# Sparsemax cross-attention on one core: thresholds by Newton steps for eight heads an operation, and score matmuls on a head's own 32 partitions

## The reference, cut to what matters

```python
def sparsemax(x):                       # over the 722 keys
    x = x - max(x); zs = sort_descending(x)
    cssv = cumsum(zs) - 1.0
    k = max(sum(zs > cssv / arange(1, L + 1)), 1)
    tau = cssv[k - 1] / k
    return clip(x - tau, 0.0)

h = layernorm(x)                        # x: 8 x 100 x 512, 16 heads of 32
q, k, v = h @ Wq + bq, ctx @ Wk + bk, ctx @ Wv + bv     # ctx: 8 x 722 x 512
att = sparsemax(q_h @ k_h.T / sqrt(32)) @ v_h           # each head h
x = x + att @ Wo + bo
h = layernorm(x)
x = x + sqrt((h @ cos(theta + theta_noise))**2 + (h @ sin(phi + phi_noise))**2)
```

## Time and profile before

| | us |
|---|---|
| median of 3 runs | 843.59 (840.98 to 843.95) |
| the profiled execution | 843.08 |
| its span, first to last instruction | 840.8 |
| TensorE busy | 657.9 (78%) |
| VectorE busy | 629.0 (75%) |
| ScalarE busy | 454.7 (54%) |
| POOL busy | 181.9 (22%) |

### The profile page before, as it was taken

The page is one execution under the profiler, slowest core; times in us unless marked ns, Lnnn a source line. Parts: engine busy times, 40 slices in busy tenths (PEclk is TensorE's granted clock), DMA queues, the critical chain, the costliest instruction groups (busy, mean ns, idle before and its releaser), DMA issues.

```text
span 840.8 us, 16547 instructions
## 1 busy us (share of the span) xinstructions
PE 657.9 (78%) x4960; PEld 423.0 (50%) x4960; DVE 629.0 (75%) x4046; ACT 454.7 (54%) x872; POOL 181.9 (22%) x147
## 2 busy tenths in 40 slices
PE   3796824778887779898888979997759979995485
PEld 2463613644466445664467536744447446742351
DVE  3699994699936997599929993899629994999401
ACT  2262745554486454874498438854538447842441
POOL 5710530002420034202420152015300152000000
PEclk9898765889889789999899989998979989997698
DMA  9610100000020000200020002000020000000000
GB/s 311 231 49 1 72 1 1 3 2 0 11 92 1 0 11 1 92 0 0 10 93 0 0 10 92 1 0 10 1 91 0 0 10 13 3 1 10 11 2 10
DMA packets 9806, 26.25 MB, mean 31 GB/s; under 512 B 2090, under 2 KB 2090, under 8 KB 8686
## 3 DMA queue, kind: packets, MB, share of 16 engines
q1 hardware_dynamic: 9710, 25.35, 8.7%
HBM read 23.71 MB, written 1.64 MB: 30 GB/s over the span
## 4 chain that ended last, share of the span: by engine, by line
DVE 70%; issue 10%; PE 8%; DMA 5%; DVEq 3%; SPq 2%; ACT 2%; ACTq 0%
DVE cand L743 22%; DVE cand L755 17%; DVE top L750 14%; DMA xq<-in_x 3%; DVE csum L765 2%; PE work L333 2%; PE work L338 2%; PE tps L406 2%; DMA out_y<-att 2%; DVE topz L761 2%; DVE gk L768 1%; SPq L193 1%; DVE g_max L771 1%; DVE st L718 1%; DVEq L830 1%
## 5 line engine op out<-in xcount | busy, mean ns | idle before, releaser
L743 DVE MAX8 cand<-S 100x8 f32<-100x60 f32 (+1 forms) x1536 | 191.0, 205 | 43.5 <-issue 25.4
L406 PE MATMUL tps<-ident,S 100*128 100x100 f32 x768 | 102.9, 276 | 80.6 <-DVEq L835 46.6
L390 PE MATMUL work<-kT,qz 128*100 128x361 f16 x768 | 151.7, 339 | 0.8 <-ACT k_f L565 0.8
L581 ACT ACTIVATE S<-S,neg_tau 100x722 f32<-100x722 f32 x128 | 114.3, 895 | 69.8 <-DVE neg_tau L773 69.8
L755 DVE MATCH_REPLACE8 cand<-top,cand 100x96 f32<-100x96 f32 x640 | 148.1, 243 | 0.0
L750 DVE MAX8 top<-cand 100x8 f32<-100x96 f32 x768 | 139.9, 245 | 0.0
L333 PE MATMUL work<-ctxT,wk 128*128 128x361 f16 x768 | 134.1, 340 | 7.0 <-ACT k_f L565 5.7
L406 PEld LDWEIGHTS tps<-ident,S 100*128 100x128 f32 x768 | 84.7, 155 | 101.2 <-ACT pT L546 44.0
L283 POOL TENSOR_TENSOR ctxT<-ctxT_f,ctxT 128x1024 f16<-128x1024 f32 (+1 forms) x24 | 46.8, 1950 | 393.1 <-ACT ctxT L546 392.8
L333 PE MATMUL work<-wv,ctxT 128*128 128x512 f16 x576 | 125.7, 379 | 0.4 <-ACT S L546 0.4
L546 ACT ACTIVATE S<-work 100x722 f32<-100x722 f32 x128 | 99.4, 776 | 27.9 <-PE work L390 25.4
(11 more groups left out here) (99 smaller groups left out, 586.5 us busy)
## 6 DMA issues: line engine op xcount, KB each, us to landing
ctxT_f<-in_ctx SPq DMA_DIRECT2D x8, 1444.0 KB, 6.7
xq<-in_x SPq DMA_DIRECT2D x8, 200.0 KB
xr<-in_x SPq DMA_DIRECT2D x8, 200.0 KB
out_y<-att SPq DMA_DIRECT2D x8, 200.0 KB
wq<-in_L_xattn_Wq SPq DMA_DIRECT2D x1, 1024.0 KB, 9.2
S<-in_L_xattn_Wk SPq DMA_DIRECT2D x1, 1024.0 KB, 11.5
S<-in_L_xattn_Wv SPq DMA_DIRECT2D x1, 1024.0 KB, 10.8
wcos<-in_L_ffn_theta SPq DMA_DIRECT2D x1, 1024.0 KB, 12.8
```

What stands on the lines that cost most here:

```text
L390: last = nc.tensor.matmul(buf[0:L, half, 0:HALF], qz2[:, i, h // G, h % G, :], kT2[:, j, h // G, half * HALF:(half + 1) * HALF], start=(n ...
L406: last = nc.tensor.transpose(tps[:, half, c * L:(c + 1) * L], S[0:L, h, kc * P:(kc + 1) * P], ident[0:L, 0:L])
L581: nc.scalar.activation(S[0:L, h, 0:N], S[0:L, h, 0:N], ACT.Relu, bias=neg_tau[:, h:h + 1], accum_out=row_sum[:, h:h + 1]).then_inc(relu_do ...
L743: last = nc.vector.max(cand[:, j, 8 * i:8 * i + 8], S[0:L, h, cuts[i]:cuts[i + 1]])
```

## The change

Thresholds are found for eight heads at once (part 0, part 1) by Newton steps from below. The start is (sum of the two largest of each piece − 1)/24; each step adds (sum of positive parts − 1)/(count of candidates not below tau), over the first 3, 5, 8 and 8 ranks of each piece. cand holds eight heads. VectorE's order becomes: maxes of group 0, mark(b−1, 1), ln1(b+1), settle(b−1, 1), maxes of group 1, Newton steps of part 0, maxes of groups 2 and 3, tail1(b−1), mark(b, 0), Newton steps of part 1, sum_squares, settle(b, 0), tail2.

The scores use q on the head's own 32 partitions (qT2, no padding), with the matmuls of two heads in turn, into both work buffers. sum_flags(b−1, 1) moves behind the transposes of head 3. ln_sd(b+1) moves behind score 7. The relus of part 0 stand at the three v_of, those of part 1 behind root and k_of 1 to 3. settle() loads one value for all eight heads and, where it is not zero, loops over them with a value load each, around one copy of refine.

```diff
             def scores(b, h):
-                if h < 2:
-                    pe.wait_ge(k_f_ready, DC * (b + 1) - 1 + h)
+                if h == 0:
+                    pe.wait_ge(k_f_ready, DC * (b + 1))
                 else:
-                    pe.wait_ge(s_ready, H * b + h - 1)
-                buf = take()
+                    pe.wait_ge(s_ready, H * b + h)
+                m = h // G
+                bufs = (take(), take())
                 for half in range(2):
                     for n, (i, j) in enumerate(((0, 0), (0, 1), (1, 0))):
-                        last = nc.tensor.matmul(buf[0:L, half, 0:HALF], qz2[:, i, h // G, h % G, :],
-                                                kT2[:, j, h // G, half * HALF:(half + 1) * HALF],
-                                                start=(n == 0), stop=(n == 2))
-                last.then_inc(work_full, 1)
+                        for head, buf in zip((h, h + 1), bufs):
+                            r = slice(DH * (head % G), DH * (head % G + 1))
+                            last = nc.tensor.matmul(buf[0:L, half, 0:HALF], qT2[r, i, m, :],
+                                                    kT2[r, j, m, half * HALF:(half + 1) * HALF],
+                                                    start=(n == 0), stop=(n == 2))
+                last.then_inc(work_full, 2)
...
                         if not first:
                             transpose_p(b - 1, g, j)
-                        scores(b, G * g + j)
-                        if g == 0 and j == 0 and not first:
+                        if j % 2 == 0:
+                            scores(b, G * g + j)
+                        if g == 0 and j == G - 1 and not first:
                             sum_flags(b - 1, 1)
...
                         s_of(b, G * g + j)
-                        if g == 0 and j == 0 and not first and not last:
+                        if g == 1 and j == G - 1 and not first and not last:
                             ln_sd(b + 1, mv1, sd1, ln1_stat, ln1_sd)
-                        if g == DC - 1 and not first:
-                            relu(b, j)
...
                 for i in range(NC // 2):
-                    if not first:
-                        relu(b, G + i)
                     v_of(b, i)
                     if not last:
                         ctxT_of(b + 1, i)
-                    if first:
-                        relu(b, i)
+                    for h in range(3 * i, min(3 * i + 3, 2 * G)):
+                        relu(b, h)
...
                     squares(b - 1)
                     root(b - 1)
                     for m in range(1, DC):
-                        relu(b, 3 * G + m - 1)
-                        if m == DC - 1:
-                            relu(b, 3 * G + m)
                         if not last:
                             k_of(b + 1, m)
+                        for h in range(2 * G + 3 * (m - 1), min(2 * G + 3 * m, H)):
+                            relu(b, h)
...
+                n = 2
+                for ranks in RANKS:
+                    E = PIECES * ranks
+                    t4 = tau_t[:, :].rearrange("p (g a c) -> p g a c", a=1, c=1)
+                    dve.wait_ge(tau_step, n)
+                    nc.vector.tensor_tensor(dif[:, :, 0:E].rearrange("p g (i r) -> p g i r", r=ranks),
+                                            pieces[:, :, :, 0:ranks], t4.broadcast_to([L, 2 * G, PIECES, ranks]),
+                                            ALU.subtract).then_inc(tau_step, 1)
+                    dve.wait_ge(tau_step, n + 1)
+                    nc.vector.tensor_scalar(over[:, :, 0:E], dif[:, :, 0:E], 0.0, None, ALU.is_ge)\
+                        .then_inc(tau_step, 1)
+                    nc.vector.tensor_scalar(dif[:, :, 0:E], dif[:, :, 0:E], 0.0, None, ALU.max).then_inc(tau_step, 1)
+                    dve.wait_ge(tau_step, n + 2)
+                    nc.vector.tensor_tensor(over[:, :, 0:E // 2], over[:, :, 0:E // 2], over[:, :, E // 2:E],
+                                            ALU.add).then_inc(tau_step, 1)
+                    dve.wait_ge(tau_step, n + 4)
+                    nc.vector.reduce_sum(count_g[:, :], over[:, :, 0:E // 2], AX).then_inc(tau_step, 1)
+                    dve.wait_ge(tau_step, n + 3)
+                    nc.vector.reduce_sum(f_sum[:, :], dif[:, :, 0:E], AX).then_inc(tau_step, 1)
...
             def one_pass(b, first, last):
 
+                steps = thresholds(b, 0)
+                next(steps)
                 if not first:
                     mark(b - 1, 1)
                 if not first and not last:
                     ln1(b + 1)
                 if not first:
                     settle(b - 1, 1)
-                thresholds(b, 0)
-                thresholds(b, 1)
-                thresholds(b, 2)
+                next(steps)
+                for _ in steps:
+                    pass
+                steps = thresholds(b, 1)
+                next(steps)
                 if not first:
                     tail1(b - 1)
                 mark(b, 0)
-                thresholds(b, 3)
+                for _ in steps:
+                    pass
```

More of the change, by code:

```diff
@@ L107, in build_kernel @@
         sq = sb("sq", [L, 2, D])
-        cand = sb("cand", [L, G, NCAND])
-        top = sb("top", [L, G, TOP])
-        topz, csum, gk = (sb(n, [L, G, TOP]) for n in ("topz", "csum", "gk"))
-        chain0, inv_k = sb("chain0", [L, G, TOP]), sb("inv_k", [L, G, TOP])
-        g_max = sb("g_max", [L, G])
+        cand = sb("cand", [L, 2 * G, NCAND])
+        dif, over = sb("dif", [L, 2 * G, NCAND]), sb("over", [L, 2 * G, NCAND], BF16)
+        tau_t, f_sum, count_g = (sb(n, [L, 2 * G]) for n in ("tau_t", "f_sum", "count_g"))
+        zero = sb("zero", [L, 1])
         neg_tau = sb("neg_tau", [L, H])
@@ L729, in ln1, with maxes @@
                            ln1_stat, ln1_sd, ln1_step, xn_ready)
[L731 to L733 removed]
+            def maxes(b, g):
                 dve.wait_ge(s_ready, H * b + G * (g + 1))
                 dve.sem_inc(scores_seen, 1)
[L738 to L774 removed]
@@ L776, in newton, with thresholds @@
-            def newton(h, n, total):
-                p = S[0:L, h, 0:N]
+                for j in range(G):
+                    for i in range(PIECES):
+                        last = nc.vector.max(cand[:, G * (g % 2) + j, 8 * i:8 * i + 8],
+                                             S[0:L, G * g + j, cuts[i]:cuts[i + 1]])
+                return last
+            def thresholds(b, part):
+                dve.sem_clear(found)
+                dve.sem_clear(tau_step)
+                maxes(b, 2 * part)
+                if part == 0:
+                    yield
+                maxes(b, 2 * part + 1).then_inc(found, 1)
+                yield
+                pieces = cand[:, :, :].rearrange("p g (i r) -> p g i r", r=8)
+                dve.wait_ge(found, 1)
+                nc.vector.tensor_reduce(f_sum[:, :], pieces[:, :, :, 0:2], mybir.AxisListType.XY,
+                                        ALU.add).then_inc(tau_step, 1)
+                dve.wait_ge(tau_step, 1)
+                nc.vector.tensor_scalar(tau_t[:, :], f_sum[:, :], -1.0, 1.0 / (2 * PIECES), ALU.add,
+                                        ALU.mult).then_inc(tau_step, 1)
+                n = 2
[12 more added lines that the diff above has]
+                    nc.vector.tensor_tensor(over[:, :, 0:E // 2], over[:, :, 0:E // 2], over[:, :, E // 2:E],
+                                            ALU.add).then_inc(tau_step, 1)
+                    dve.wait_ge(tau_step, n + 4)
+                    nc.vector.reduce_sum(count_g[:, :], over[:, :, 0:E // 2], AX).then_inc(tau_step, 1)
+                    dve.wait_ge(tau_step, n + 3)
+                    nc.vector.reduce_sum(f_sum[:, :], dif[:, :, 0:E], AX).then_inc(tau_step, 1)
+                    dve.wait_ge(tau_step, n + 5)
+                    nc.vector.tensor_scalar(count_g[:, :], count_g[:, :], 1.0, None, ALU.max).then_inc(tau_step, 1)
+                    dve.wait_ge(tau_step, n + 7)
+                    nc.vector.reciprocal(count_g[:, :], count_g[:, :]).then_inc(tau_step, 1)
+                    dve.wait_ge(tau_step, n + 8)
+                    nc.vector.scalar_tensor_tensor(f_sum[:, :], f_sum[:, :], -1.0, count_g[:, :], ALU.add,
+                                                   ALU.mult).then_inc(tau_step, 1)
+                    dve.wait_ge(tau_step, n + 9)
+                    nc.vector.tensor_tensor(tau_t[:, :], tau_t[:, :], f_sum[:, :], ALU.add).then_inc(tau_step, 1)
+                    n += 10
+                dve.wait_ge(tau_step, n)
+                nc.vector.tensor_scalar(neg_tau[:, 2 * G * part:2 * G * (part + 1)], tau_t[:, :], -1.0, None,
+                                        ALU.mult).then_inc(tau_ready, 1)
@@ L875, in angles @@
                 dve.sem_inc(angle_ready, 1)
-            nc.vector.memset(chain0[:, :, 1:TOP], 1.0)
-            nc.vector.memset(chain0[:, :, 0:1], 0.0)
```

(6 more changed lines are left out.)

120 lines of the change are left out of this document (32 added, 88 removed).

## The result

The changed kernel takes 967.64 us (median of four runs, 965.6 to 971.03) against 843.77 for the kernel before beside it: ratio 1.148, 95% interval 1.143 to 1.152. The forecast was 935 us, range 880 to 990. The profiled execution took 967.81 us, with a span of 966.0 us; its granted clock averages 0.781, against 0.886 before. An execution over 1.5% above the fastest of its kernel counts as slow and is left out of the ratios; the profiled one of the packed scores alone (879.95 us) was such a one, so no line of it is compared.

A forecast was written before the change was run, and what follows sets the result against it. VectorE bounds 70% before; afterwards handoff waits make a pass 102.0 us for 88.9. First pass 142.9, six passes 612.0, refinements 46.7, last pass 131.4, outside 2.3: 935 us, range 880 to 990.

The forecast's parts named there:

- Handoff through mark: Pass start: TensorE's sum_flags and the mix behind it wait for mark, queued behind 48 maxes on VectorE: 6.8 us.
- Score 7: End of group 1's scores: cold mix, transposes and first pair, second pair warm, 11.0 us more, reached at 17.8.
- Settle: ln_sd, ln1 and settle(b−1, 1) behind score 7, value load and branch 3.0 us: verdict at 23.5.
- Rival 2: TensorE stays fast in stalls, settle()'s branch short: 5.9 + 1.8 less a pass, 880; opposite 955; chance 0.10.
- Score 15: Groups 2 and 3 wait for settle's verdict, TensorE cold again, 8.9 + 7.4 us: reached at 39.9.
- Pair of scores: Score matmuls of two heads on different 32 partitions run side by side on TensorE: 0.92 us a pair.
- Newton: VectorE's threshold steps for eight heads: 16.1 us a run, part 1's run with nothing beside it.
- Behind the root: ScalarE's three k_of and eight relus of part 1 after the root: 11.5 us.
- First pass: From the start, with maxes behind the angle loads, to zero of pass 1 at 142.9 us.
- Rival 1: Row tiles don't overlap, pairs of scores cost 1.84 us: about 9.6 more a pass, 1000; chance 0.17.
- Rival 3: VectorE's work sets the pass after all, 9.3 us less a pass: about 770; chance 0.06.
- Rival 4: Thresholds fall short on the chip, each refined head some 9 us more, 1040 at a dozen; chance 0.02.

The follow-up runs named there:

- the packed scores alone: The kernel before with only the packed score matmuls added, its thresholds and order kept: 867.86 us, ratio 1.025.
- the 855.46 us run: The changed kernel with mark, ln1, settle(), sum_flags and ln_sd back in their earlier places, padded q and one head at a time: 855.46 us, ratio 1.014.

## Why the prediction was right, and what it mis-sized

The direction, the place and the mechanism held; the time was 33 us short. It lies in the stated range, but 3 us above the band of 900 to 965 that had most of the chance. Zero is the moment when score 3 is copied; I take the first maxes for it, 503.26 in the pass shown.

- Handoff through mark: forecast 6.8 us to the mix, measured 6.3 (509.58, with sum_flags at 509.35), with TensorE released by mark as foretold. The runs put a price on it by itself: 43 us.
- Score 7: forecast 17.8, measured 18.5 (its copy, from 520.96 on, ends at 521.7). The cold rows were taken rightly: 1.26 for six transposes. But the second pair, forecast warm, was cold too (2.04).
- Settle: forecast 23.5, measured 22.2 (525.43). The branch cost 1.18 us of "issue", the low end of 1.2 to 4.1; I had taken 3.0. Rival 2's second half was right in this and was worth 1.8 us for each branch on the path.
- Score 15: forecast 39.9, measured 41.5, and from the verdict on 19.3 us for 16.4. This is the step that failed in its reason. I let the clock return within each stretch of groups, because I ascribed its fall to idle time. Groups 2 and 3 ran at half clock from 525.22 to about 538 with TensorE idle for 0.6 us of it. With the padded q in the same order (956.22) the clock does return: from the verdict to the end of the last mix it is 16.2 us there (523.43 to 539.64) and 20.2 in after (525.22 to 545.42). The prediction had this as the variant of rival 2 (3 us more a pass, 955) and gave as its reason that TensorE is less dense. The run with 32 rows and one head at a time shows another one: score matmuls on few rows bring the low clock without any idle time.
- First value projection: 44.3, measured 46.0 (549.28); relus of part 0: 63.6, measured 65.2.
- Pair of scores: forecast 0.92 us to the next transposes, measured 1.06 (541.56 to 542.62). The prediction had no row for what a change to row tiles costs; it is the 0.14 us of the run with 64 rows.
- Newton: forecast 16.1 us a run. The first run took 15.5: steps of 2.6, 3.4, 4.5 and 4.5 us for 2.6, 3.4, 4.6 and 4.6. The double rate of tensor_scalar held with bf16 output too (0.56 us for 768 elements). The second run took 18.0. "Newton of part 1 with nothing beside it" was wrong: there was GpSimd's split of q and k, which I had put "off the path". The run with that work moved gives 15.5. The Trainium skill, "SBUF — State Buffer" (section "Who interferes with whom"), says that a tensor_scalar at double rate or a tensor_tensor with both inputs in SBUF and a GpSimd operation exclude each other for their whole length, and a reduce doesn't; the rows agree (reduces beside GpSimd kept 0.40 and 0.64 us, in the first pass of the 855.46 us run), and the page should have been weighed in the prediction.
- Behind the root: 11.5 forecast, 11.5 measured (three k and eight relus, from 589.5 to 601.0). Table load and group 0: 8.4, measured 8.7.
- First pass: zero of pass 1 at 142.9, measured 147.5; its second Newton run had GpSimd beside it nearly all the way and took 21.3 us for 16.1. Refinements: three, as the arithmetic on the inputs had said, 18.4, 16.3 and 9.8 us for 18, 18 and 10.7.
- Sum: 4.6 us for zero of pass 1, 27 for six passes (4.6 each, 1.3 more in one of them, less 2 on the refinements) and 2 for the last pass. The 4.6 us of a pass are themselves a balance: some 4 too few for the clock and the changes to row tiles together and 2.5 too few for mark and Newton beside GpSimd, 2 too many for the branch; that two of the errors had opposite signs is luck.
- "VectorE does 9 us less and stands about 30 us": the first half holds, the second was a slip. 102.0 less the 61.5 us of work leave 40, and the trace has 44.9 (106.63 less 61.77).

Rival 1 (tiles don't overlap) fell by the rows of 12 matmuls in 1.12 us at full clock. Rival 3 (faster, 770, if the handoffs met work that is ready) can be judged by the run with all handoffs restored: 855 us. Its price was wrong, as VectorE's 9.3 us of saved work don't come off the pass: eight relus and three k on ScalarE behind the second Newton run, and GpSimd's hold on that run, take their place. Rival 4 fell: three heads are refined.

## What to carry to other kernels

When an operation is moved ahead of another on one engine, follow what stands behind it on the others: mark, ln_sd and settle cost nothing by their own length (0.15, 0.29 and 0.3 us), and their places in the queues cost 83 of the 124 us lost (101 with the padded scores). Before small work goes to one side as "off the path", look at which engine's work will be critical beside it in the new order: GpSimd's splits of q lay beside maxes before, which they don't hold, and beside Newton steps after, which they do. Using fewer rows of TensorE's array for the same columns is no saving of time by itself, costs some 0.14 us at each change between such matmuls and 128-row ones, and can cost the clock.

## What the runs showed of the hardware

- The granted clock fell with the rows of the array in use: with 128, 64 and 32 rows in the score matmuls it averages 0.886, 0.843 and 0.752 (843.8, 863.0, 934.0 us), with TensorE busy 39.67 of 40 us in the last. How much of the first step is due to the changes of the next item isn't shown. The Trainium skill, "TensorE: Matmul & The Clock Gate" (section "What's actually happening"), says that the clock is set by how busy the engine has been; by busy time the run with 32 rows should have had the full clock, and the measurement decides.
- A change between 128-row transposes and score matmuls on 64 or 32 rows costs TensorE some 0.14 us: 0.66 us for 0.52 one way and 1.06 for 0.92 the other at the full clock (64 rows), 1.19 for 1.05 and 1.98 for 1.81 at half clock (32 rows).
- Two heads on different 32 rows run side by side: 12 matmuls in 1.12 us at 2.4 GHz and 2.04 at 1.2 GHz, and six of one head 2.04 at 1.2 GHz.
- An operation of GpSimd holds tensor_scalar and tensor_tensor operations of VectorE until it ends, 0.5 to 1.4 us each time; reduces beside one kept their time (0.40, 0.64), and so did the maxes of 96 beside the nine operations on q in the kernels with the old thresholds (0.72 for four). A Newton run of 15.5 us became 18.0 with three of them beside it, 21.3 with ten.
- A value load with a branch over eight copies of a long body cost 4.1 to 4.4 us, over one copy 1.2 (1.18 at 525.43).
